# A mixture-of-experts network on one core: the shared expert's first unit moved ahead of a branch, both gate parts in one product, and a second token half of 312 columns

## The reference

```python
x = x + gnn(layernorm(x), edges, W, b)
h = layernorm(x) @ lin0_w + lin0_b
h = silu(h @ swi1_w1 + b1) * (h @ swi1_w2 + b2)
scores = softmax(h @ gate_w.T)                       # gate_w: 8 experts x 1024
topv, topi = top_k(scores, 4); topv /= sum(topv)
routed = sum over experts e of combine[:, e] * ((silu(h @ exp_w1[e]) * (h @ exp_w3[e])) @ exp_w2[e])
shared = (silu(h @ sh_w1) * (h @ sh_w3)) @ sh_w2     # hidden width 2048
h = (routed + shared) @ lin1_w + lin1_b
h = silu(h @ swi2_w1 + c1) * (h @ swi2_w2 + c2)
return x + h
```

## Time and profile before

| what | value |
|---|---|
| median of 3 runs | 1620.05 us (1615.27 to 1620.29) |
| the profiled execution | 1616.77 us |
| its span, first to last instruction | 1614.8 us |
| PE busy | 1590.5 us, 98% |
| PE weight loads busy | 1574.9 us |
| POOL, ACT, DVE busy | 831.8, 520.8, 468.0 us |
| share of PE in the chain that ended last | 95% |
| mean granted TensorE clock | 0.996 |
| instruction packets of queue q8 | 88, 1.44 MB |

### The profile page before, as it was taken

How to read it: one execution, slowest core, us unless ns; L and a number is a source line. 1 busy time by engine, 2 the same in 40 slices (tenths; PEclk the granted TensorE clock), 3 DMA queues, 4 the chain that set the end, 5 groups by cost and what they waited for, 6 DMA issues and landing times.

```text
span 1614.8 us, 28323 instructions
## 1 busy us (share of the span) xinstructions
PE 1590.5 (98%) x11032; PEld 1574.9 (98%) x11032; DVE 468.0 (29%) x869; ACT 520.8 (32%) x750; POOL 831.8 (52%) x701
## 2 busy tenths in 40 slices
PE   7999999999999999999999999999999899999999
PEld 7998999999999999999999999999999899999998
DVE  8654411122620112324141322424211154111011
ACT  5323232222222333343444344444444222222210
POOL 2311133333443666867677686868677566333331
PEclk9999999999999999999999999999999999999999
DMA  4411122223232445546455555646455566233221
GB/s 132 129 40 51 66 92 79 66 81 114 68 112 79 135 136 162 173 138 204 144 187 157 178 171 160 192 144 213 145 185 164 153 181 180 79 103 107 76 85 32
DMA packets 65251, 205.62 MB, mean 127 GB/s; under 512 B 13498, under 2 KB 15373, under 8 KB 65143
## 3 DMA queue, kind: packets, MB, share of 16 engines
q1 hardware_dynamic: 44530, 156.85, 32.3%
q0 software_dynamic: 14976, 32.81, 6.5%
q10 hardware_dynamic: 5637, 14.35, 2.7%
HBM read 185.01 MB, written 18.95 MB: 126 GB/s over the span
## 4 chain that ended last, share of the span: by engine, by line
PE 95%; DVE 1%; ACT 1%; POOL 1%; DMA 1%; issue 1%; ACTq 0%; SPq 0%; POOLq 0%; DVEq 0%
PE acc L1407 88%; PE acc L1387 2%; PE acc L1697 1%; PE acc L1676 1%; POOL w_lo L409 1%; DMA rows<-x_dram 1%; PE acc L1454 0%; DVE yrow L836 0%; ACT act_b L565 0%; POOL gath L470 0%; PE acc L1478 0%; PE acc L1463 0%; PE acc L1745 0%; PE acc L1558 0%; ACT act_b L570 0%
## 5 line engine op out<-in xcount | busy, mean ns | idle before, releaser
L409 POOL TENSOR_TENSOR w_lo<-raw,w_hi 128x512 fp32r<-128x512 f32 x592 | 757.4, 1305 | 689.2 <-ACT w_hi L399 682.6
L1407 PE MATMUL acc<-act_b,w_hi 128*128 128x314 f32 (+8 forms) x2560 | 567.9, 311 | 0.0
L1407 PE MATMUL acc<-act_x,w_hi 128*128 128x344 f32 (+7 forms) x2048 | 451.7, 309 | 3.1 <-POOL w_lo L409 2.5
L1407 PEld LDWEIGHTS acc<-act_b,w_hi 128*128 128x128 f32 x2560 | 425.7, 189 | 0.0
L1407 PE MATMUL acc<-act_a,w_hi 128*128 128x314 f32 x1792 | 397.1, 311 | 5.5 <-issue 5.5
L1407 PE MATMUL acc<-act_b,w_lo 128*128 128x314 f32 (+8 forms) x1280 | 394.4, 308 | 0.0
L1407 PEld LDWEIGHTS acc<-act_x,w_hi 128*128 128x128 f32 x2048 | 342.3, 188 | 4.7 <-issue 4.0
L399 ACT ACTIVATE w_hi<-raw 128x1024 fp32r<-128x1024 f32 x296 | 310.6, 1050 | 39.1 <-PE acc L1407 26.9
L1407 PE MATMUL acc<-act_x,w_lo 128*128 128x344 f32 (+7 forms) x1024 | 316.4, 309 | 0.0
L1407 PEld LDWEIGHTS acc<-act_a,w_hi 128*128 128x128 f32 x1792 | 300.2, 190 | 5.7 <-issue 5.7
L1407 PE MATMUL acc<-act_a,w_lo 128*128 128x314 f32 x896 | 276.8, 309 | 0.0
(11 more groups left out here) (199 smaller groups left out, 861.9 us busy)
## 6 DMA issues: line engine op xcount, KB each, us to landing
raw<-stream_dram SPq DMA_DIRECT2D x296, 512.0 KB, 3.7
y_dram<-yrow POOLq DMA_DIRECT2D x16, 512.0 KB
rows<-x_dram ACTq DMA_DIRECT2D x2, 2500.0 KB
y_dram<-yrow POOLq DMA_DIRECT2D x8, 352.0 KB
x_dram<-rows ACTq DMA_DIRECT2D x5, 500.0 KB
h_rows_dram<-rows ACTq DMA_DIRECT2D x1, 2500.0 KB
rows<-x_dram SPq DMA_DIRECT2D x3, 448.0 KB
out_dram<-rows ACTq DMA_DIRECT2D x1, 1120.0 KB
```

The lines of the kernel that those rows point to most:

```text
L409: last = nc.gpsimd.tensor_tensor(w_lo[:, s, c], raw[:, s, c], w_hi[:, s, c].bitcast(f32), ALU.subtract)
L1407: ins = pe.matmul(o, w, xs_[h], start=(first and w is hi and xs_ is x_hi), stop=(last and w is lo))
```

## The change

The last expert gets its own call in PE's program. Ahead of it the register with the largest count is loaded; within it, between the last two `turn_y`, the first unit of shb is computed; the branch follows, and behind it shb starts with its second unit. In the general path the banks 0 and 1 are replaced by 2 and 3, since bank 0 and 1 then hold the first unit's result. The gate's high and low parts stand side by side, 16 columns per step k, so that one matmul gives both parts' logits: 8 steps of 2 products in 2 halves; DVE adds the two parts in `route_scores`. The second half of the tokens is 312 columns wide in all general layers (`HL`); the other engines still read 314, whose last two columns of a bank DVE clears once at the start.

```diff
+HL = T - HT + 1
...
-        gate_hi = act_x[:, 0, 0:D]
-        gate_lo = act_x[:, 1, 0:D]
-        logits_t = gath[0:EXPERTS, D:D + TP]
+        gate_cols = gate_raw.rearrange("p (k n) -> p k n", n=P)[:, :, 0:EXPERTS]
+        gate_both = act_x[:, 0, 0:KC * GW].rearrange("p (k n) -> p k n", n=GW)
+        logits_t = gath[0:GW, D:D + TP]
...
         def _(dve):
+            dve.memset(acc[:, :, HL:HT], 0.0).then_inc(psum_zero, 1)
...
-                lo = acc[0:TT, TPB + 2, 0:NT * EXPERTS].rearrange("p (i e) -> p i e", e=EXPERTS)
-                link(dve.tensor_reduce(col1[0:TT, :], lo, AX.X, ALU.max))
+                parts = acc[0:TT, TPB + 2, 0:NT * GW].rearrange("p (i e) -> p i e", e=GW)
+                link(dve.tensor_copy(lg[0:TT, :, :], parts[:, :, 0:EXPERTS]))
+                link(dve.tensor_tensor(lg[0:TT, :, :], lg[0:TT, :, :], parts[:, :, EXPERTS:GW], ALU.add))
+                link(dve.tensor_reduce(col1[0:TT, :], lg[0:TT, :, :], AX.X, ALU.max))
...
         def _(pe):
+            pe.wait_ge(psum_zero, 1)
...
                 for h, b in enumerate(banks):
+                    n = HL if h == 1 else width
                     for k in range(KC):
-                        xx = [[t[:, k, h * width:(h + 1) * width]] for t in (x_hi, x_lo)]
-                        last = products([acc[:, b, 0:width]], w_hi[:, s, k * P:(k + 1) * P],
+                        xx = [[t[:, k, h * width:h * width + n]] for t in (x_hi, x_lo)]
+                        last = products([acc[:, b, 0:n]], w_hi[:, s, k * P:(k + 1) * P],
...
-            def gated(st, x_hi, x_lo, first_ready, after=None, freed=None):
+            def gated(st, x_hi, x_lo, first_ready, after=None, freed=None, begun=False):
...
-                    dense(st.base, 2 * m, x_hi, x_lo, first_ready if m == 0 else None)
+                    if m >= 1 or not begun:
+                        dense(st.base, 2 * m, x_hi, x_lo, first_ready if m == 0 else None)
...
-                    outs = [acc[:, TPB + h, 0:HT] for h in range(2)]
                     for k in range(KC):
-                        xx = [[t[:, k, h * HT:(h + 1) * HT] for h in range(2)] for t in (a_hi, a_lo)]
-                        last = products(outs, gate_hi[:, k * P:(k + 1) * P], gate_lo[:, k * P:(k + 1) * P],
-                                        xx[0], xx[1], k == 0, k == KC - 1)
+                        for t in (a_hi, a_lo):
+                            for h, n in enumerate((HT, HL)):
+                                last = pe.matmul(acc[0:GW, TPB + h, 0:n], gate_both[:, k, :],
+                                                 t[:, k, h * HT:h * HT + n], start=(k == 0 and t is a_hi),
+                                                 stop=(k == KC - 1 and t is a_lo))
...
                     if nxt:
                         expert_in(e + 1, m)
+                if not nxt:
+                    pe.wait_ge(yt_copied, e * KC + KC - 2)
+                    dense(U_SHB, 0, a_hi, a_lo)
                 turn_y(e, KC - 1)
...
-            for e in range(EXPERTS):
-                expert(e, e < EXPERTS - 1)
+            for e in range(EXPERTS - 1):
+                expert(e, True)
+            over = fullest(pe)
+            expert(EXPERTS - 1, False)
...
-            with pe.If(fullest(pe) > CAP):
+            with pe.If(over > CAP):
...
-            pe.wait_ge(yt_copied, EXPERTS * KC)
-            gated(shb, a_hi, a_lo, None, shb_extra)
+            gated(shb, a_hi, a_lo, None, shb_extra, begun=True)
```

More of the change, by code:

```diff
@@ L200, in build @@
         const_ready = sem("const_ready")
+        psum_zero = sem("psum_zero")
         ident_zero = sem("ident_zero")
@@ L706, in _ @@
             act.wait_ge(gate_loaded, 16)
-            act.activation(gate_hi, gate_raw, ACT.Copy).then_inc(gate_split, 1)
+            act.activation(gate_both[:, :, 0:EXPERTS], gate_cols, ACT.Copy).then_inc(gate_split, 1)
             for m in range(KC):
@@ L775, in _ @@
                             load_unit(m * 2 + 1, n * UNITS_EXPERT + m * 2 + 1)
-                            act.activation(silu[:, 0:OV_SLOTS], acc[:, 0, 0:OV_SLOTS], ACT.Silu).then_inc(ov_silu, 1)
+                            act.activation(silu[:, 0:OV_SLOTS], acc[:, 2, 0:OV_SLOTS], ACT.Silu).then_inc(ov_silu, 1)
                             act.wait_ge(ov_prod, n * KC + m + 1)
@@ L781, in _ @@
                             load_unit(m + UNITS_UP, n * UNITS_EXPERT + m + UNITS_UP)
-                            act.activation(prod[:, 1, 0:OV_SLOTS], acc[:, 0, 0:OV_SLOTS], ACT.Copy).then_inc(ov_yt, 1)
+                            act.activation(prod[:, 1, 0:OV_SLOTS], acc[:, 2, 0:OV_SLOTS], ACT.Copy).then_inc(ov_yt, 1)
                 act.wait_ge(ov_added, 2 * NT)
@@ L1038, in _ @@
             dve.wait_ge(gate_split, 1)
[L1039 removed]
+            dve.tensor_tensor(gate_both[:, :, EXPERTS:GW], gate_cols, gate_both[:, :, 0:EXPERTS].bitcast(f32),
+                              ALU.subtract).then_inc(gate_split, 1)
             def h_rows(m):
@@ L1431, in half_unit @@
                 s = off % RING
+                n = (HT, HL)[h]
                 pe.wait_ge(hi_split, u + off + 1)
@@ L1436, in half_unit @@
                         between(k)
-                    xx = [[t[:, k, h * HT:(h + 1) * HT]] for t in (x_hi, x_lo)]
-                    last = products([acc[:, bank, 0:HT]], w_hi[:, s, k * P:(k + 1) * P],
+                    xx = [[t[:, k, h * HT:h * HT + n]] for t in (x_hi, x_lo)]
+                    last = products([acc[:, bank, 0:n]], w_hi[:, s, k * P:(k + 1) * P],
                                     w_lo[:, s, k * P:(k + 1) * P], xx[0], xx[1], k == 0, k == KC - 1)
@@ L1639, in sha_extra @@
                     for i in range(NT):
-                        last = pe.transpose(acc[0:TT, TPB + 2, i * EXPERTS:(i + 1) * EXPERTS],
-                                            logits_t[:, i * TT:(i + 1) * TT], ident[0:EXPERTS, 0:EXPERTS])
+                        last = pe.transpose(acc[0:TT, TPB + 2, i * GW:(i + 1) * GW],
+                                            logits_t[:, i * TT:(i + 1) * TT], ident[0:GW, 0:GW])
                     last.then_inc(logits_done, 1)
```

14 lines of the change are left out of this document (8 added, 6 removed).

## The result

| | before | after |
|---|---|---|
| median | 1619.57 us (1615.27 to 1620.29, 4 runs) | 1607.24 us (1606.59 to 1608.65, 4 runs) |
| profiled execution | 1616.77 us | 1606.59 us |
| its span | 1614.8 us | 1604.9 us |

The ratio is 0.9931, with a 95% interval of 0.9916 to 0.9946: 11.2 us, or 8.7 to 13.6. The forecast was 1608.5 within 1603.5 to 1614.

The account below looks back on a forecast made before the run. The prediction took PE, 95% of the chain, as the bound. Savings of 7.74, 2.36 and 2.2 less 0.73 gave 11.6 us, from the 1620.05 median to 1608.5 us; range 1603.5 to 1614.

Parts of the forecast that it names:

- part 1: Last expert on PE: with shb's first unit ahead of the branch, nothing idles; 7.74 us saved.
- part 2: Register load moved ahead of the eighth expert, where PE's line is tight: 0.73 us lost.
- part 3: Gate on PE: 32 matmuls instead of 48, at 0.1454 us each; 2.36 us saved.
- part 4: Second half of general layers and gate: two columns less in 2512 matmuls, 0.44 ns a column; 2.2 us saved.
- two covers: At the branch: PE's sequencer runs 2.4 us ahead of the array, and the instruction packet is there before the branch.
- further behind the packet's place: Branch on PE stands 66 instructions, about 4.8 us of products, later, so its packet is there and PE need not idle.
- the case that nothing idles: Behind the last turn_y at the branch: PE has no idle time, 7.74 us saved; forecast as it stands, chance 0.50.
- The end I had named for 0: Register load ahead of the eighth expert: loss of 0 if handled while the sequencer stands at the wait.
- The rival with the clock falling behind it: Gate: the 16-column product loads the array too little and the clock falls; price 1.6 us, 1610, chance 0.09.
- The bounds of 0 and 3.8: Saving in us from 312 columns: 0 from the last units' 0.1458 us a matmul, 3.8 from 314's 0.1453 against 312's 0.1438.
- The first tile's slack: Late in shb: DVE's last weighted sum after the gathers ends at 1297, PE wants it at 1301.1; 4 us of slack.
- The slower rival: In shb, POOL's save of the last expert becomes PE's wait; 1625 us or more, chance 0.02.

Follow-up runs that it names:

- late load: Changed kernel with the register load back at the branch, behind the unit and the last turn_y: 1606.50 us, ratio 0.9931; repeated 1606.75 us, ratio 0.9931.
- the unit behind: Changed kernel with shb's first unit and the register load back behind the branch, gate product and 312 columns kept: 1613.79 us, ratio 0.9968.
- 236 ahead: Kernel before with 236 increments of an unread semaphore in PE's queue up to the branch, nothing else changed: 1617.51 us in one execution.
- 304 columns: Changed kernel with the second half 304 wide from shb on: 1609.2 us in one execution.
- 296 columns: Changed kernel with the second half 296 wide from shb on: 1603.7 us in one execution.

## Why the prediction was right, point by point

| term | forecast, us | measured, us |
|---|---|---|
| part 1, unit ahead of the branch | 7.74 | 7.71 (shb's first two units, 22.29 to 14.58) |
| part 2, register load | -0.73 | -0.78 |
| part 3, gate | 2.36 | 2.44 (the unit with it, 13.98 to 11.54) |
| part 4, 312 columns | 2.2 | 1.05 |
| sum | 11.6 | 10.4 |

**Part 1** came out as worked. Of its two covers the first, the sequencer's lead of 2.4 us, was right and is now measured by itself (3.78 us of branch, 1.32 idle). The second, why the branch would be short at the new place, was half right. That it waited for a packet of instructions, and that a shift of 66 instructions would free it, holds: 66 idle instructions alone do it. But "further behind the packet's place" is not the rule. By my reasoning 236 instructions would have been as good, and they gave the whole hole back; and the gate's edit without the unit moves the branch to where it is short and PE stalls two matmuls behind it (0.85 and 4.10 us). The step that failed is the one that looked at the branch's own packet and not at its target's. The new place, 70 instructions in, happened to be good by either rule.

I took the case that nothing idles since a jump costs nothing where the instructions are at hand; the rows on ACT carried that, and 0.36 us on PE confirms it in size.

**Part 2** was right, for the reason given: PE's line is tight there. It is a loss that needn't be: behind a unit queued ahead, the load costs nothing. The end I had named for 0 is that of the late load, not of this place.

**Part 3** was right; 16 columns of weights and 314 moving ones run at 0.143 us. The rival with the clock falling behind it did not come.

**Part 4** is the term that was mis-sized: 1.05 us for 2.2. The slope of 0.44 ns a column over 316 to 296 is there from 312 down (0.47). But it was carried over a step in which these rows already contradicted each other, 314 standing above 316 and 312 at the end standing at 0.1458. The bounds of 0 and 3.8 held it. The lower one rested on a misread row: 3.50 us for 24 matmuls is a piece that borders on transposes at both ends, and where units of this expert follow each other with nothing between, one takes 3.43 us, 0.1431 a matmul. And 1.05 is what the slower of the two paces of 312 gives; at the quicker one a unit loses 0.026 us instead of 0.007, against the 0.021 of the forecast.

**What could come late.** The first tile's slack was forecast at 4 us and was 3.9 (sum done at 1295.04, PE at 1298.96). The fifth tile I did not look at, and there it is between 0.06 and 4.0. The slower rival, POOL's save, did not appear: PE has no wait on L1417 in shb.

**The total.** The terms fell 1.2 us short of the forecast, and the medians moved by 12.3 us, the ratio's middle 11.2. The difference is within the spread of the first stage; nothing of it should be put down to the change. That the total came so close to the forecast is therefore part luck.

## What to carry to other kernels

Where an engine idles with "issue" at a jump, count its instructions: a jump over more than a packet of 256 cost PE up to 5.5 us here, and the clock behind it. It cost 0.9 us, with the register load ahead of it, where it stood 30 or 70 behind its packet's start and its target well ahead of the end of the next. The 30 sufficed with a wait of 2.7 us between; in plain products, 4.6 us are an estimated 63 instructions (4.6 / 0.073). A few idle instructions upstream move it there, and any edit upstream (here 32 instructions less at the gate) can move it away, so a gain or loss of this size from a harmless edit should first be checked against the packets. Queue work ahead of a jump or a register load: the sequencer's lead hides 2.4 us of it, and right behind a wait for another engine it hides nothing.

## What the runs showed of the hardware

- The stall for instructions need not show in the branch's record: 362 ns of branch and 4.10 us idle two matmuls later.
- 66 increments of a semaphore, six behind a unit, cost PE nothing.
- The clock fell in the three kernels in which PE stood for 4.1 us or more at the branch (before, the unit behind, 236 ahead) and not behind 0.9 to 1.3 us. Between them it went both ways: at the wait for the last sum it fell behind 1.9 us (304 columns) and not behind 2.9 us (296 columns). At half clock the unit costs 1.6 us more.
- The same loop with halves of 314 and 312 columns has two paces, 6.973 and 6.954 us a unit, at the same granted clock.
- A sum on DVE (125x1024) that begins while POOL's split runs takes 2.13 us instead of 1.28. Where POOL's split begins within the sum, the sum stays at 1.28.
